# A two-layer graph network: the second layer's table by rows of 26 nodes, and 23 of 80 edge columns fetched by TensorE

## The reference

```python
s_src = h @ attn_w[:d]
s_dst = h @ attn_w[d:]
e = s_src[src] + s_dst[dst]
e = jnp.where(e >= 0, e, LEAKY_SLOPE * e)
m = jax.ops.segment_max(e, dst, num_segments=N)
ex = jnp.exp(e - m[dst])
denom = jax.ops.segment_sum(ex, dst, num_segments=N)
alpha = ex / denom[dst]
out = jax.ops.segment_sum(h[src] * alpha[:, None], dst, num_segments=N)
...
x = _layernorm(x + _L1_gnn_ref(x, L1_gnn_attn_w, src, dst), axis=-1)
```

## Time and profile before

| | |
|---|---|
| median of 3 runs | 4680.36 us (4677.33 to 4682.39) |
| the profiled execution | 4683.32 us, span in the trace 4681.6 us |
| mean granted clock of TensorE | 0.923 |
| second layer's loop, first gather to last | 2878.2 to 4512.4 us |

### The profile page before, as it was taken

The page is one execution under the profiler, slowest core; times in us unless marked ns, Lnnn a source line. Parts: engine busy times, 40 slices in busy tenths (PEclk is TensorE's granted clock), DMA queues, the critical chain, the costliest instruction groups (busy, mean ns, idle before and its releaser), DMA issues. The chain is left out here.

```text
span 4681.6 us, 64944 instructions
## 1 busy us (share of the span) xinstructions
PE 3269.9 (70%) x20039; PEld 1947.3 (42%) x20039; DVE 3037.6 (65%) x5153; ACT 1853.1 (40%) x3061; POOL 3391.2 (72%) x3518
## 2 busy tenths in 40 slices
PE   0005888888888888888888002989899898988840
PEld 0001333233333233332332002878788787777740
DVE  4525999999999999999998220444444444444432
ACT  3003555555555555555554002444333444444300
POOL 5776777777777777777774675777777777777766
PEclk9999999999999999999999555999999999999975
DMA  9512222222222222222221001222222222222211
GB/s 328 156 36 44 46 47 52 45 46 51 45 46 53 45 46 52 45 45 54 45 45 28 16 19 37 59 58 57 64 64 64 64 64 64 60 56 57 64 28 26
DMA packets 271524, 271.70 MB, mean 58 GB/s; under 512 B 183168, under 2 KB 237896, under 8 KB 268737
## 3 DMA queue, kind: packets, MB, share of 16 engines
q1 hardware_dynamic: 161988, 194.83, 15.2%
q0 software_dynamic: 109024, 72.30, 10.0%
q10 hardware_dynamic: 462, 4.00, 0.3%
HBM read 180.54 MB, written 90.34 MB: 58 GB/s over the span
## 5 line engine op out<-in xcount | busy, mean ns | idle before, releaser
L607 POOL DMA_INDIRECT edge<-xp_d,idx x1440 | 1416.0, 983 | 537.8 <-issue 391.1
L1194 POOL DMA_INDIRECT gxb<-tab_d,idxb x1200 | 1249.6, 1041 | 388.4 <-issue 339.9
L859 DVE TENSOR_TENSOR prod<-G_ps,hid 128x1000 f32<-128x1000 f32 x1200 | 1400.5, 1195 | 124.2 <-PE G_ps L742 109.4
L742 PE MATMUL G_ps<-FT,wst 32*128 32x500 f32 x4800 | 896.6, 633 | 369.6 <-DVE prod L859 368.4
L1260 PE MATMUL G_ps<-tb,hot 125*126 125x500 f32 (+1 forms) x3200 | 681.3, 368 | 390.7 <-ACT hotk L1218 313.1
L1260 PEld LDWEIGHTS G_ps<-tb,hot 125*126 125x126 f32 x3200 | 574.4, 199 | 466.9 <-issue 313.3
L771 PE MATMUL R_ps<-prod,red 128*32 128x500 f32 x4800 | 589.4, 594 | 0.0
L742 PEld LDWEIGHTS G_ps<-FT,wst 32*128 32x128 f32 x4800 | 246.3, 183 | 805.7 <-DVE prod L859 754.0
L663 ACT ACTIVATE hid<-T_ps 128x500 f32<-128x500 f32 x400 | 233.2, 583 | 721.6 <-PE T_ps L762 701.2
L762 PE MATMUL T_ps<-FT,wst 32*128 32x500 f32 x800 | 432.3, 620 | 3.1 <-ACT FT L659 3.1
L1280 DVE TENSOR_REDUCE gxb<-G_ps 125x20 f32<-125x500 f32 (+1 forms) x400 | 212.5, 581 | 322.8 <-PE G_ps L1263 317.8
(11 more groups left out here) (245 smaller groups left out, 4567.3 us busy)
## 6 DMA issues: line engine op xcount, KB each, us to landing
edge<-sel_d SPq DMA_DIRECT2D x80, 546.9 KB
xd_d<-zeros SPq DMA_DIRECT2D x16, 1562.5 KB, 29.0
y_d<-zrb SPq DMA_DIRECT2D x40, 595.0 KB
edge<-xp_d,idx POOLq DMA_INDIRECT x1440
xv<-xd_d SPq DMA_DIRECT2D x40, 560.0 KB
y_d<-zr SPq DMA_DIRECT2D x40, 560.0 KB
gxb<-tab_d,idxb POOLq DMA_INDIRECT x1200
em<-in_edge_attr SPq DMA_DIRECT2D x40, 175.0 KB
```

The lines of the kernel that those rows point to most:

```text
L607: nc.gpsimd.indirect_dma_start(out=edge_c[:, i, 8:8 + DIM], out_offset=None, in_=xp_d, in_offset=bass.IndirectOffsetOnAxis(col, 0)).then_i ...
L742: return Tn.matmul(G_ps[pair][:, a * 512:a * 512 + GW], wst[rows, r * 128:(r + 1) * 128], FT[k][rows, :], start=True, stop=True)
L859: V.tensor_tensor(prod[b][i][:, :].rearrange("p (a e) -> p a e", a=2), gv, hid[k][:, :].rearrange("p (a e) -> p a e", a=1).broadcast_to([1 ...
L1194: nc.gpsimd.indirect_dma_start(out=gx[h][:, c * T1:(c + 1) * T1], out_offset=None, in_=tab_d, in_offset=bass.IndirectOffsetOnAxis(idx[h][: ...
```

## The change

The table's row gets 26 nodes (`KL`); 481 rows hold the 12500 nodes and 6 zeros. Three groups have 128 rows, the last 97, which lie in partitions 31 to 127; partitions 0 to 30 of this group hold the penalty, so that the one-hot for k is part of the last group's one-hot. A column is then 8 pairs of matmuls, of 17 x 26 = 442 and 16 x 26 = 416 columns, and `far` and `hotk` go. To bring the table into this layout it is written to `tab_d` first, read back by rows of 26 nodes into `tbl`, and split from there. TensorE gets 11 columns of a chunk with h = 0 and 12 of one with h = 1, POOL 29 and 28. The waits within POOL's chunk are gone. The node numbers for the last group come by four loads, of 96, 1, 16 and 15 rows.

```diff
-    XC = 10
-    CG = C - XC
+    XCS = (11, 12)
+    XCP = sum(XCS)
+    CGS = tuple(C - w for w in XCS)
     NG4 = 4
-    KL = 25
-    XP = XC * P
-    FU = 20
-    GS = KL * (DIM + 1) + 1
+    KL = 26
+    HI = -(-N // KL)
+    R3 = 31
+    XPS = tuple(w * P for w in XCS)
+    XPM = max(XPS)
+    FU = 17
+    GS = KL * (DIM + 1)
...
+    def cols_before(ch, h, t):
+        return t * XCP + (XCS[0] if h else 0)
...
-                        if i > 0:
-                            low_part(i - 1)
-                    low_part(NPIECE - 1)
+                    for i in range(NG4):
+                        low_part(i)
...
-                        act.wait_ge(S("c_x1e"), i + 1)
+                    act.wait_ge(S("c_far"), 2)
+                    act.wait_ge(S("c_tbl"), 16 * NG4 + 16)
+                    for i in range(NG4):
                         nc.scalar.activation(by_feature(tb[0], i), by_node(i), ACT.Copy).then_inc(S("c_hi"), 1)
...
-                    sp.wait_ge(S("c_tab"), 32)
+                    sp.wait_ge(S("c_tab"), 48)
+                    sp.wait_ge(S("c_far"), 2)
+                    for i in range(NG4):
+                        lo = R3 if i == NG4 - 1 else 0
+                        hi = 127 if i == NG4 - 1 else 128
+                        sp.dma_start(tbl[lo:hi, i * GS:(i + 1) * GS],
+                                     tab_d.rearrange("(r k) f -> r (k f)", k=KL)[i * 128:i * 128 + hi - lo, :]).then_inc(S("c_tbl"), 16)
+                    sp.dma_start(tbl[127:128, (NG4 - 1) * GS:], tab_d.rearrange("(r k) f -> r (k f)", k=KL)[HI - 1:HI, :]).then_inc(S("c_tbl"), 16)
...
-                        for a, t in ((0, nodes[h]), (1, nodek[h])):
-                            rows = sel_d[a].rearrange("i p -> (i p)")[bass.ds(ch * XP, XP)].rearrange("(a f) -> a f", a=1).broadcast_to([t.shape[0], XP])
-                            by_rows(sp, t, rows, S(f"d_nd{h}"))
+                        hi, k = [sel_d[a].rearrange("i p -> (i p)")[bass.ds(cols_before(ch, h, t) * P, XPS[h])].rearrange("(a f) -> a f", a=1) for a in range(2)]
+                        sp.dma_start(nodes[h], hi.broadcast_to([128, XPS[h]])).then_inc(S(f"d_nd{h}"), 16)
+                        for a, r0, r1 in ((hi, R3, 127), (hi, 127, 128), (k, 0, 16), (k, 16, R3)):
+                            sp.dma_start(nodek[h][r0:r1], a.broadcast_to([r1 - r0, XPS[h]])).then_inc(S(f"d_nd{h}"), 16)
...
                             if not (first and h == 0):
-                                pool.wait_ge(S("d_col"), (t * 2 + h) * XC - 1)
+                                pool.wait_ge(S("d_col"), cols_before(t * 2 + h, h, t) - 1)
                                 pool.sem_inc(S("go"), 1)
-                            for c in range(CG):
-                                if c % 3 == 0 and c > 3:
-                                    pool.wait_ge(S("d_col"), (t * 2 + h) * XC + c // 3 - 1)
-                                    pool.sem_inc(S("go"), 1)
+                            for c in range(CGS[h]):
...
                         for l in range(2):
                             for g in range(NG4):
                                 for (f0, f1, w), ps in zip(FUS, slot):
-                                    nc.tensor.matmul(ps[0:PE2, 0:w], hot[h][:, g * XP + j * P:g * XP + j * P + PE2],
-                                                     tb[l][:, g * GS + f0 * KL:g * GS + f0 * KL + w], start=(l == 0 and g == 0), stop=False)
-                        for (f0, f1, w), ps in zip(FUS, slot):
-                            last = nc.tensor.matmul(ps[0:PE2, 0:w], hotk[h][:, j * P:j * P + PE2], far[:, 0:w], start=False, stop=True)
+                                    last = nc.tensor.matmul(ps[0:PE2, 0:w], hot[h][:, g * XPS[h] + j * P:g * XPS[h] + j * P + PE2],
+                                                            tb[l][:, g * GS + f0 * KL:g * GS + f0 * KL + w], start=(l == 0 and g == 0), stop=(l == 1 and g == NG4 - 1))
                         last.then_inc(S("d_col"), 1)
```

More of the change, by code:

```diff
@@ L185, in gnn_resnorm_kernel @@
             tn = sbt("tn", [P, 4 * NP])
-            NSEL = 2 * PAIRS * XC
+            NSEL = PAIRS * XCP
             SELB = NSEL // 4
-            iot_i = sbt("iot_i", [P, NG4], i32)
-            ssel, psel, ksel, gsel = [sq[:, a * NSEL:(a + 1) * NSEL] for a in range(4)]
+            iot_i = sbt("iot_i", [128, NG4], i32)
+            iot_s = sbt("iot_s", [128, 1])
+            ssel, psel, ksel = [sq[:, a * NSEL:(a + 1) * NSEL] for a in range(3)]
             selT = [blkbuf[0:SELB, a * 4 * P:(a + 1) * 4 * P] for a in range(2)]
@@ L992, in gnn_resnorm_kernel @@
         both = ExitStack()
-        tb = [both.enter_context(nc.sbuf_tensor(f"tb{l}", [P, NG4 * GS], f32r)) for l in range(2)]
-        far = both.enter_context(nc.sbuf_tensor("far", [P, FU * KL], f32r))
-        assert NG4 * KL == NP and KP == KL and NPIECE == NG4
+        tb = [both.enter_context(nc.sbuf_tensor(f"tb{l}", [128, NG4 * GS], f32r)) for l in range(2)]
         with ExitStack() as st:
@@ L1120, in gnn_resnorm_kernel @@
             NS = len(SLOTS)
-            assert 2 * XC % NS == 0
-            ab = [sbt(f"ab_{g}", [P, XP]) for g in range(2)]
-            niot = sbt("niot", [P, NG4])
+            LATE = XCP % NS
+            assert LATE == NS - 1 and XCS[0] >= LATE
+            ab = [sbt(f"ab_{g}", [128, XPM]) for g in range(2)]
+            niot = sbt("niot", [128, NG4])
             sdr = two("sdr", C)
@@ L1267, in _ @@
                         for h in range(2):
-                            for j in range(XC):
-                                column(t * 2 + h, h, j)
+                            for j in range(XCS[h]):
+                                column(t * 2 + h, h, j, t)
                 @block.vector
@@ L1330, in _ @@
                     for h in range(2):
[L1331 to L1335 removed]
+                        V.memset(hot[h][:, NG4 * XPS[h]:].bitcast(f32), 0.0).then_inc(S("d_init"), 1)
+                    dve.wait_ge(S("d_init"), 7)
+                    for j in range(XCS[0]):
+                        pick(0, 0, j, 0)
                     with dve.Fori(0, PAIRS - 1) as t:
@@ L1338, in _ @@
                             chunk(h, t)
-                            for j in range(XC):
-                                pick(t * 2 + h + 1, 1 - h, j)
+                            for j in range(XCS[1 - h]):
+                                pick(t * 2 + h + 1, 1 - h, j, t + h)
                     chunk(0, PAIRS - 1)
-                    for j in range(XC):
-                        pick(2 * PAIRS - 1, 1, j)
+                    for j in range(XCS[1]):
+                        pick(2 * PAIRS - 1, 1, j, PAIRS - 1)
                     chunk(1, PAIRS - 1)
```

114 lines of the change are left out of this document (56 added, 58 removed).

## The result

The changed kernel takes 4599.63 us (4596.27 to 4600.41, 4 runs), the kernel before 4679.9 beside it: 80.3 us less, ratio 0.9827 (95% interval 0.981 to 0.9844). The forecast was 4604 us with a range of 4588 to 4624.

What follows compares the result with a forecast made beforehand. POOL's issuing of gathers was taken as the bound. Fewer gathers (-73.7 us) and an earlier start (-2.2) took 4681.6 to 4605.4; with 1.7 around the span 4607.1, less 3.0 to the median 4604 us, range 4588 to 4624.

Steps and rivals of the forecast that it cites:

- The bound: Second layer's loop: POOL's issue of gathers sets the pace, 40.45 us a chunk before the change.
- The gathers: Second layer's loop: 59 fewer gathers in chunks 1 to 39 at 1.249 us each, -73.7 us; lengthening stays with the chunk.
- The start of the loop: Chunk 0 of the second layer: TensorE starts as before, POOL resumes after column ten at 2933.6, -2.2 us.
- TensorE's column: Second layer's loop: eight pairs take 3.17 us for 3.43; 0 on the path, TensorE taking over at 3.36.
- Half clock: TensorE in the second layer's loop: half-clock columns come only after a wait of some 4 us; covered, 0 us.
- Loads: Node-number loads in the second layer's loop: five a chunk for four, about 8.5 us, cover of 9 us; 0.
- The table: Table stage: written to DRAM, read back and split, done by 2785; cover 75 us, 0 within 1 us.
- one-hots and picks: Second layer's loop: eight ScalarE activations for ten, hidden by some 14 us; VectorE's picks 4% larger; each 0.
- The stages ahead: Set-up and table stages ahead of the second layer's loop: changes there covered, 0 us.
- Rival A: Second layer's loop: POOL stays the bound but the stretch per chunk changes, 4588 to 4616; chance with the main forecast 0.80.
- A's other side: Second layer's loop: the stretch grows by 0.3 us a chunk, 4616; sign: gathers over 3 us beside VectorE's product.
- The profiled run: Whole kernel: the profiled run, 4683.3, lies 3.0 us above the median of three, so the forecast becomes 4604.

Runs made afterwards that it cites:

- x10: The changed kernel with 10 columns of every chunk by TensorE and 30 gathers by POOL; 4666.1 us, ratio 0.9967 to the kernel before.
- onehalf: The changed kernel with half of TensorE's work, the products with the table's low part left out; 4576.03 us (one run).
- b_nowait: The kernel before with only the waits inside POOL's gather loop left out; 4676.46 us against 4679.21, ratio 0.9996.
- x12: The changed kernel with 12 columns of every chunk by TensorE and 28 gathers by POOL; 4593.6 us, ratio 0.9813 to the kernel before.
- b_x12: The kernel before with 12 columns of every chunk by TensorE, still nine pairs each, and 28 by POOL; 4707.99 us, ratio 1.0063.
- rows97: The changed kernel with the last group's node numbers loaded by two transfers of 97 and 31 rows in place of four; 5159.74 us (one run).
- late: The changed kernel with two small VectorE copies ahead of each chunk's product; 4575.78 us, ratio 0.9774 to the kernel before.
- split2: The changed kernel with VectorE's product of a chunk done in two halves; 4560.27 us, ratio 0.9742 to the kernel before.
- prod2: The changed kernel with VectorE's product of a chunk done twice, once into a tile that nothing reads; 4614.09 us (one run).
- split4_ng: The changed kernel with VectorE's product in four parts and without POOL's chunk-head wait for columns; 4526.47 us, ratio 0.967 to the kernel before.

## Why the prediction came out right

**The bound.** POOL was the bound and stayed it: gathers put back cost time (x10), TensorE's work halved gives the start and little more (onehalf). b_nowait shows that the waits inside the chunk were not what held it.

**The gathers.** Forecast 59 x 1.249 = 73.7 us, measured 73.1. That these agree needed a lengthening that stays, and it did, 2.99 us a chunk before and after. It need not have: in x10, with the cheaper column and 30 gathers, it was 2.85, and counted from there the same 59 gathers are 67.4 us. The prediction had no term for how TensorE's work changes the product's length, and between these two kernels there was none to pay. The choice that mattered was to price a gather at the bare 1.249 and to leave the lengthening with the chunk; at 1.34 each it would have been 79. The runs back the choice and sharpen its reason. The rule of the Trainium skill (SBUF — State Buffer, section "SBUF: two separate sides") that GpSimd cannot write descriptors while VectorE holds the port was read rightly as a price per VectorE instruction, and the times agree; no run here tells the port from another cause. What I had not seen is that the price is the rest of the one instruction met, plus some 0.66 us before the gather ends. The same section of the Trainium skill says that whichever of the two starts first holds the port for its whole instruction, and the earlier trace rows held it already.

**The start of the loop.** Forecast 2.2 us, measured 4.6: the term that was mis-sized. Timelines: the loop's first instruction on POOL in the kernel before, then in the changed kernel the same on POOL, the first one-hot on ScalarE and the first column on TensorE:

```profile
2875.12 0.19 POOL L1182 MEMSET idxb<- 128x40 int32 x2 [10.14 <-POOLq L1014]
...
2868.36 0.19 POOL L1202 MEMSET idxb<- 128x40 int32 x2 [10.19 <-POOLq L1025]
...
2878.68 2.77 ACT L1230 ACTIVATE ab<-edge,niot 128x1375 f32<-128x1375 f32 x2 [121.37 <-DMA edge<-sel_d]
...
2889.86 5.30 PE L1276 MATMUL G_ps<-tb,hot 128*126 128x442 f32 x15 [308.52 <-ACT hot L1234]
```

The columns from there to POOL's resuming took 34.6 us, as forecast, 2.2 less than before. TensorE was to start as late as before; it started at 2889.86, 21.5 us behind the loop's first POOL instruction for 23.9 before, and these are the other 2.4 us. The eight one-hot activations took 11.2 us as worked out (2878.68 to 2889.86), so the 1.75 us saved on ScalarE were real, and the loads did not cost the 1.6 that I put against them: ScalarE began 10.3 us behind that instruction for 11.0 before.

**TensorE's column.** Forecast 3.17 us, limit 3.36. Timeline of TensorE, the first matmul of a column and of the next:

```profile
3743.06 0.36 PE L1276 MATMUL R_ps<-tb,hot 128*126 128x442 f32 x1
...
3746.21 4.08 PE L1276 MATMUL G_ps<-tb,hot 128*126 128x442 f32 x20
```

3.15 us. Where TensorE never waits it is 3.14 (x12, 37.65 us for 12 columns) and 3.41 with nine pairs (b_x12, 40.93), so the old column was taken 0.02 too long and the new one 0.03. An estimate from these two: 6864 and 7434 output columns at 2.4 GHz are 2.86 and 3.10 us, and what is left is 35 ns a pair in both. Shrinking it by output columns alone left this part out, at no cost here.

**Half clock.** Forecast: only behind a wait, covered. In the changed kernel TensorE waits once a pair, its granted clock is 0.50 (1.2 GHz) from 3707 to 3710 us, behind such a wait of 2.2 us, and 1.00 (2.4 GHz) again from 3711 to 3714, and that column takes 4.8 us (3706.88 to 3711.66) for 3.15. It costs nothing while POOL paces.

**Loads.** Forecast 8.5 us, measured about 7; the cover held, and rows97 shows what stood behind it. **The table** was ready at 2759.3 us, forecast 2785, with 100 us of cover left; **one-hots and picks** cost nothing, as forecast (a column's picks 1.12 us). **The stages ahead** came out 6.8 us shorter in the profiled run, for 0 forecast; 2.9 in the mean, and the part of it that is the change stays open, since kernels with the same lines there differ by 5.3.

**Rival A.** Its better side, 17 us, rested on the gather of chunk 0 that took 2.15 us: chunks that picks let go would have the same. 16 chunks were let go by picks, and the lengthening stayed at 3.0 us a chunk. But in 36 of 39 chunks the gather still began 2.3 to 2.6 us behind L1313, just inside the product, which starts 2.25 behind it; in the other three it was 3.5, with 2.15 us for the gather. That the phase stayed where it was, the prediction could not know: here it had luck, within its range. The sign named for A's other side, gathers of more than 3 us beside the product, was there (up to 3.34 us, 3.17 in the median), but so it was before (up to 3.25, 3.14), and it told nothing. The mechanism existed, the phase did not come by itself; late and split2 brought it by hand, for 24 and 39 us.

**The profiled run** lay, as taken into the sum, close to its median (4597.3 + 1.7 against 4599.6), before 3.0 above it. That correction of 3 us stands for scatter of the stages ahead of the loop. The sum itself has a slip of 0.3 us: 4681.6 - 75.9 is 4605.7 and not 4605.4.

## What to carry to other kernels

When the engine that issues indirect transfers is the bound, price its transfers at the bare distance between two of them, and look separately at which VectorE instruction each lengthened one meets: cut that instruction, or move its start behind a transfer's, before trying to make VectorE faster. A change that takes work from the bound is worth its full price only while the next engine's step stays below the new period, so work out that limit first (3.36 us a column here). Take a kernel with the work put back (x10) beside the change: it showed 5.5 us of another effect that the plain comparison hid. Compare traces from a common point inside the stage that was changed: here the stages ahead scattered by 5 us with no edit in them.

## What was not expected of the hardware

A gather that begins beside a VectorE product ends 0.65 to 0.71 us behind that instruction's end, if 0.27 us or more of it are left (0.81 to 0.84 us behind the extra product of prod2). For products of 2.69, 1.44, 1.49 and 0.79 us the lengthened gathers took up to 3.34, 2.07, 2.27 and 1.38 us in place of 0.94. One that began 0.25 us ahead of the product took 0.95. More VectorE work (late) or the same in more instructions (split2, split4_ng) made the kernel faster. The product of 1280 elements took 2.50 us while TensorE was idle and 2.69 while it worked (x10, onehalf and the changed kernel); why is open. The same product took 1.49 us written in order and 2.69 with a stride. Loads of 128, 97 and 31 rows took 32 us, in rows of 128, 96, 16, 15 and 1 they took 7. In x12 and b_x12, the kernels with 28 gathers in every chunk, POOL stood 2.0 and 2.2 us behind the first gather of every fourth chunk, with no releaser in the trace; its cause is open.
